# Routed activations of an expert layer: turned on VectorE and spread by ScalarE, where TensorE transposed them

## The reference, cut to what matters

```python
logits = xt @ W_router + routing_bias
scores, idx = jax.lax.top_k(jax.nn.sigmoid(logits), 2)
g = jnp.einsum('th,ehi->tei', xt, Wg_r)
u = jnp.einsum('th,ehi->tei', xt, Wu_r)
hmid = silu(g) * u
combined = jnp.einsum('tei,eih,te->th', hmid, Wd_r, wts)
```

## Time and profile before

| | us |
|---|---|
| median of 3 runs | 812.71 (811.16 to 813.40) |
| profiled execution, its own time | 809.95 |
| span from first to last instruction in it | 808.1 |
| PE busy in the span | 773.6 |
| DVE busy | 517.4 |
| ACT busy | 355.5 |
| POOL busy | 301.0 |

### The profile page before, as it was taken

The page is one execution under the profiler, slowest core; times in us unless marked ns, Lnnn a source line. Parts: engine busy times, 40 slices in busy tenths (PEclk is TensorE's granted clock), DMA queues, the critical chain, the costliest instruction groups (busy, mean ns, idle before and its releaser), DMA issues.

```text
span 808.1 us, 17427 instructions
## 1 busy us (share of the span) xinstructions
PE 773.6 (96%) x6752; PEld 574.0 (71%) x6753; DVE 517.4 (64%) x1125; ACT 355.5 (44%) x913; POOL 301.0 (37%) x157
## 2 busy tenths in 40 slices
PE   4799999999899999989999999899999999999996
PEld 3555455554657778878867877788888888888884
DVE  5799798788652447777788887855364333443335
ACT  4356545661443248852178768523432122211221
POOL 1000000000442833732032213533649999993034
PEclk9999999999899999999999999999999999999999
DMA  9968756683520050040388000030485355531138
GB/s 341 390 252 327 259 218 243 262 326 122 219 105 1 0 149 13 2 138 0 105 312 314 1 0 1 22 137 25 183 306 210 112 206 167 191 135 52 52 114 275
DMA packets 46576, 127.04 MB, mean 157 GB/s; under 512 B 4001, under 2 KB 8353, under 8 KB 40369
## 3 DMA queue, kind: packets, MB, share of 16 engines
q1 hardware_dynamic: 36752, 105.44, 35.9%
q10 hardware_dynamic: 7200, 12.32, 4.4%
q0 software_dynamic: 2560, 8.39, 3.1%
HBM read 101.99 MB, written 24.15 MB: 156 GB/s over the span
## 4 chain that ended last, share of the span: by engine, by line
PE 81%; DVE 5%; DMA 5%; POOL 3%; ACT 3%; issue 2%; SPq 0%; DVEq 0%; ACTq 0%; POOLq 0%
PE scores L611 11%; PE bank L641 11%; PE bank L1137 7%; PE bank L1139 7%; PE bank L1138 7%; DMA nat<-in_ctx_keys 3%; PE bank L691 2%; POOL picked L1379 2%; PE bank L845 2%; PE bank L693 2%; PE bank L851 2%; PE bank L692 2%; PE bank L846 2%; PE bank L626 2%; PE bank L881 2%
## 5 line engine op out<-in xcount | busy, mean ns | idle before, releaser
L1844 DVE STREAM_TRANSPOSE ctxT<-nat 128x1024 f32<-128x1024 f32 (+3 forms) x124 | 116.9, 1004 | 7.8 <-DMA nat<-in_ctx_keys 7.5
L641 PE MATMUL bank<-nat,probT 128*64 128x512 f32 (+1 forms) x416 | 93.9, 597 | 0.1
L1366 POOL TENSOR_TENSOR ring_lo<-ring_raw,ring_hi 128x2048 fp32r<-128x2048 f32 x18 | 83.0, 4611 | 14.5 <-ACT ring_hi L1732 13.3
L1244 POOL TENSOR_TENSOR wq_lo<-wq_raw,wq_hi 128x1024 fp32r<-128x1024 f32 x4 | 9.3, 2352 | 207.6 <-ACT wq_hi L1477 207.6
L1137 PE MATMUL bank<-ring_hi,xg_lo 128*128 x180 | 74.2, 412 | 0.0
L1139 PE MATMUL bank<-ring_hi,xg_hi 128*128 x180 | 70.6, 392 | 0.0
L1138 PE MATMUL bank<-ring_lo,xg_hi 128*128 x180 | 70.1, 389 | 0.0
L2488 DVE TENSOR_TENSOR rhm_lo<-bank,rhm_hi 128x512 fp32r<-128x512 f32 x21 | 14.5, 692 | 80.2 <-ACT rhm_hi L1743 80.2
L641 PEld LDWEIGHTS bank<-nat,probT 128*64 128x64 f32 (+1 forms) x416 | 27.9, 136 | 51.6 <-issue 48.1
L1749 ACT COPY hn<-bank 128x512 f32<-128x512 f32 x22 | 12.9, 588 | 112.0 <-PE bank L1139 112.0
L611 PE MATMUL scores<-ctxT,hn 32*64 32x416 f32 (+8 forms) x1536 | 55.2, 426 | 5.1 <-issue 2.7
(11 more groups left out here) (317 smaller groups left out, 1936.1 us busy)
## 6 DMA issues: line engine op xcount, KB each, us to landing
nat<-in_ctx_keys SPq DMA_DIRECT2D x48, 1024.0 KB, 8.1
ring_raw<-in_Wexp SPq DMA_DIRECT2D x21, 1024.0 KB, 6.3
x_slots<-zeros SPq DMA_DIRECT2D x1, 5632.0 KB, 18.2
y_slots<-zeros SPq DMA_DIRECT2D x1, 5632.0 KB, 32.7
hn<-x_slots ACTq DMA_DIRECT2D x22, 256.0 KB, 4.5
y_slots<-hn ACTq DMA_DIRECT2D x22, 256.0 KB, 3.0
w_raw<-in_Wexp SPq DMA_DIRECT2D x3, 1024.0 KB, 5.3
nat<-in_ctx_keys SPq DMA_DIRECT2D x16, 130.0 KB
```

What stands on the lines that cost most here:

```text
L641: last = nc.tensor.matmul(context_bank(k)[64 * b:64 * b + 64, :], probT[0:n, j, 64 * b:64 * b + 64], nat[k % 2][0:n, b, j, :], start=j == ...
L1366: last = nc.gpsimd.tensor_tensor(ring_lo[at], ring_raw[at], ring_hi.bitcast(F32)[at], ALU.subtract)
L1844: dve.transpose(dst, src).then_inc(columns_ready, 1)
```

## The change

For tiles 0 to 20 PE no longer transposes the hidden tile. Instead:

- DVE turns the 32x32 blocks of `rhm` with one STREAM_TRANSPOSE into `rhm_blocks`, straight behind the multiplication.
- ACT places the 16 blocks of rows and columns with 16 copies of 32 partitions x 4x32 elements into `rhmT`. They stand ahead of `output_rows(t - 1)`, where the one cast out of bank 3 stood behind it.
- DVE makes the high part with `tensor_copy` from `rhmT` (SBUF to SBUF), having waited also for `rdown_full` of tile t-1, and the low part with a TENSOR_TENSOR whose two inputs both lie in SBUF.

The last tile, 21, is done as before, through bank 3.

The core of the diff:

```diff
             def routed_hidden(t, par, at, turn=None):
-                if not (isinstance(t, int) and t < 2):
-                    hidden_columns(t - 1)
                 pe.wait_ge(xgT_ready, t + 1)
...
-                    if isinstance(t, int) and t == 1 and m == gate:
-                        hidden_columns(0)
...
             def hidden_columns_out(t):
-                act.wait_ge(rhmT_full, t + 1)
-                nc.scalar.copy(hidden_parts(t)[0][:].rearrange("p c q -> p (c q)"), bank[3][:]).then_inc(rhm_split, 1)
+                act.wait_ge(rhm_turned, 2 * t + 1)
+                if isinstance(t, int) and t == TILES - 1:
+                    last = nc.scalar.copy(rhm_last[0][:].rearrange("p c q -> p (c q)"), bank[3][:])
+                else:
+                    for g in range(4):
+                        for a in range(4):
+                            last = nc.scalar.copy(rhmT[B32 * a:B32 * (a + 1), :, B32 * g:B32 * (g + 1)],
+                                                  rhm_blocks[B32 * g:B32 * (g + 1), :, a, :])
+                last.then_inc(rhm_split, 1)
...
             def routed_step(t, par, turn, load=True):
...
-                    output_rows(t - 1, 1 - par, turn)
-                    hidden_columns_out(t)
+                hidden_columns_out(t)
+                output_rows(t - 1, 1 - par, turn)
...
                 dve.tensor_tensor(rhm[:], rhm[:], bank[2][:], ALU.mult).then_inc(rhm_ready, 1)
+                if not (isinstance(t, int) and t == TILES - 1):
+                    dve.wait_ge(rhm_ready, t + 1)
+                    dve.transpose(rhm_blocks[:].rearrange("p c a q -> p (c a q)"), rhm[:]).then_inc(rhm_turned, 1)
...
             def hidden_split(t):
                 dve.wait_ge(rhm_split, t + 1)
...
+                if not (isinstance(t, int) and t == 0):
+                    dve.wait_ge(rdown_full, t)
+                dve.tensor_copy(rhm_hi[:], rhmT[:]).then_inc(rhm_turned, 1)
+                dve.wait_ge(rhm_turned, 2 * t + 2)
+                dve.tensor_tensor(rhm_lo[:], rhmT[:], rhm_hi.bitcast(F32)[:], ALU.subtract).then_inc(rhmT_ready, 1)
```

More of the change, by code:

```diff
@@ L300, in perceiver_kernel @@
         rhm = place(172, "rhm", [P, D])
+        rhm_blocks = place(156, "rhm_blocks", [P, HC, 4, B32])
+        rhmT = place(158, "rhmT", [P, HC, P])
         rhm_hi = place(174, "rhm_hi", [P, HC, P], F32R)
@@ L348, in perceiver_kernel @@
         xg_loaded, y_stored = ([sem(f"{n}{i}") for i in range(2)] for n in ("xg_loaded", "y_stored"))
-        xgT_full, xg_split, xgT_ready, rgate_full, rup_full, rsilu_ready, rhm_ready, rhmT_full, rhm_split, rhmT_ready, rdown_full, yo_ready = (
-            sem(n) for n in ("xgT_full", "xg_split", "xgT_ready", "rgate_full", "rup_full", "rsilu_ready", "rhm_ready", "rhmT_full",
+        xgT_full, xg_split, xgT_ready, rgate_full, rup_full, rsilu_ready, rhm_ready, rhm_turned, rhm_split, rhmT_ready, rdown_full, yo_ready = (
+            sem(n) for n in ("xgT_full", "xg_split", "xgT_ready", "rgate_full", "rup_full", "rsilu_ready", "rhm_ready", "rhm_turned",
                              "rhm_split", "rhmT_ready", "rdown_full", "yo_ready"))
@@ L1161, in routed_hidden, with last_hidden_columns @@
                     routed_product(bank[b], m, at, xg_hi[par], xg_lo[par], full)
-                    if isinstance(t, int) and t == 1 and m == gate:
-                        hidden_columns(0)
                     if m == gate and turn is not None:
                         rows_columns(t + 1, 1 - par, turn)
[L1167 to L1172, removed]
+            def last_hidden_columns():
+                pe.wait_ge(rhm_ready, TILES)
                 for c in range(HC):
                     last = nc.tensor.transpose(bank[3][:, c * P:(c + 1) * P], rhm[:, c * P:(c + 1) * P], ident)
-                last.then_inc(rhmT_full, 1)
+                last.then_inc(rhm_turned, 1)
             def routed_output(t, par, at):
@@ L1223, in _ @@
             routed_hidden(TILES - 1, 1, at[1])
-            hidden_columns(TILES - 1)
+            last_hidden_columns()
             routed_output(TILES - 2, 0, at[0])
@@ L1765, in _ @@
             routed_silu(1)
+            hidden_columns_out(1)
             output_rows(0, 0, 0)
-            hidden_columns_out(1)
             def routed_step(t, par, turn, load=True):
@@ L1773, in routed_step @@
                 routed_silu(t)
-                if isinstance(t, int) and t == TILES - 1:
-                    hidden_columns_out(t)
-                    output_rows(t - 1, 1 - par, turn)
-                else:
-                    output_rows(t - 1, 1 - par, turn)
-                    hidden_columns_out(t)
+                hidden_columns_out(t)
+                output_rows(t - 1, 1 - par, turn)
             act.wait_ge(slots_ready, 4)
@@ L2483, in routed_mult @@
                 dve.tensor_tensor(rhm[:], rhm[:], bank[2][:], ALU.mult).then_inc(rhm_ready, 1)
+                if not (isinstance(t, int) and t == TILES - 1):
+                    dve.wait_ge(rhm_ready, t + 1)
+                    dve.transpose(rhm_blocks[:].rearrange("p c a q -> p (c a q)"), rhm[:]).then_inc(rhm_turned, 1)
             def hidden_split(t):
                 dve.wait_ge(rhm_split, t + 1)
-                hi, lo = hidden_parts(t)
-                dve.tensor_tensor(lo[:].rearrange("p c q -> p (c q)"), bank[3][:],
-                                  hi.bitcast(F32)[:].rearrange("p c q -> p (c q)"), ALU.subtract).then_inc(rhmT_ready, 1)
+                if isinstance(t, int) and t == TILES - 1:
+                    hi, lo = rhm_last
+                    dve.tensor_tensor(lo[:].rearrange("p c q -> p (c q)"), bank[3][:],
+                                      hi.bitcast(F32)[:].rearrange("p c q -> p (c q)"), ALU.subtract).then_inc(rhmT_ready, 1)
+                    return
+                if not (isinstance(t, int) and t == 0):
[3 more added lines that the diff above has]
+                dve.tensor_tensor(rhm_lo[:], rhmT[:], rhm_hi.bitcast(F32)[:], ALU.subtract).then_inc(rhmT_ready, 1)
             rows_columns_out(0, 0)
```

## The result

The changed kernel takes 873.46 us (median of 4 runs, 872.31 to 877.43), the kernel before 812.56 (811.16 to 813.4) on the same chip: 1.076 times as long, interval 1.0722 to 1.0798, or some 61 us more. The forecast was 881, range 834 to 900. The profiled execution took 872.87 us with a span of 871.1, 8 us under the sum.

A forecast was written before the change was run, and what follows sets the result against it. PE bounds the kernel before, at 9.11 us a tile; afterwards the DVE-ACT circle does. 602.2 to the first multiplication, 191.9 for 19 circles, 6.5, exclusions 46, then 32.7 and 1.85 make 881 us; 8-in-10 range 834 to 900.

The forecast's parts named there:

- the circle: DVE and ACT, from one tile's multiplication to the next: a closed chain of 10.10 us, longer than PE's 8.67.
- the exclusion: DVE's high and low part and POOL's splits exclude each other for whole instructions: 6.2 us a hit tile, 46 us in all.
- PE's transposes: Four on PE per hidden tile, 0.44 us; removing 21 times four, 9.2 us, gains nothing as PE stops being the bound.
- the upper bound, 17.5: Longest circle of a hit tile: four POOL instructions per circle, 17.5 us, 7.4 us more than the unhit circle.
- the bursts' edges: POOL's splits come in about four bursts of six; waits falling away where bursts begin or end take off 8 us.
- The turn and the multiplication: On DVE beside POOL: each reads one SBUF tensor, so priced at no wait; 18 us more if the turn waited too.
- From the multiplication of tile 19 to ACT's copy: End of the routed part: 6.5 us to ACT's copy of tile 18's product, with 32.7 us behind it.
- PE's clock: Rival: PE, idling 7 us in a 16 us circle, may fall to 1.2 GHz; adds nothing unless it lasts through the tile.
- no exclusion: Rival: DVE's high and low part do not wait for POOL's instructions; 835 us, chance 0.10.
- Overlapping copies: Rival: ACT's 16 copies overlap, 3.3 us for all; 848 us with exclusion, chance 0.10; 806 us without, chance 0.04.
- a wait in one request only: Rival: only one of DVE's two requests per tile waits for POOL, 25 us; 860 us, chance 0.09.
- passed over a second time: Rival: DVE is passed over at a POOL instruction boundary, each request waiting about twice, 76 us; 911 us, chance 0.07.

The follow-up runs named there:

- e2: Changed kernel with the turned hidden tile in PSUM bank 3, where ACT's copies write and DVE's high and low part read: 835.7 us, 1.0254 of before.
- e4: Kernel before, PE transposes kept, but ACT copies bank 3 to SBUF and DVE makes both parts from there: 853.89 us, 1.0445 of before.
- e6: e2 with PE turning the next rows ahead of the gate product and DVE making input rows while it waits for the copies: 817.69 us, 1.0079 of before.
- e7: e6 with ACT loading the input rows one step earlier, right after the SiLU: 817.66 us, 1.0077 of before.
- e10: e7, tile 18's product stored ahead of tile 19's copies, DVE's weight-split wait moved to the previous tile's turn, which PE's gate awaits: 807.31 us, 0.994 of before.
- e3: Changed kernel with ACT storing the previous tile's down product ahead of the 16 copies, except for the last tile: 928.03 us, 1.1398 of before.
- e9: e7, tile 18's product stored ahead of tile 19's copies, weight-split wait moved from DVE to PE ahead of the gate product: 811.78 us, 0.9998 of before.
- e5: Changed kernel with the edits of e2 and e3 together: 837.37 us, 1.0314 of before.
- e1: Changed kernel with each POOL split of a 128x2048 weight matrix made by four 128x512 instructions: 849.74 us, 1.0418 of before.

## Why the prediction was right

The mechanism was the forecast one, in both halves; e2 and e4 show the halves apart, and e6 that the circle is what sets the pace. The size of one half, the exclusion, was off by 8.5 us of 46.

- PE's transposes were called worth nothing while the circle is longer. Right: the circle of a quiet tile is 10.0 or 10.4 us. Once the circle is shorter (e6, e7, e10) the tile takes 8.62 us; the forecast figure for that was 8.67.
- The circle, 10.10 us forecast. By its terms at 735.90: multiplication, turn and handovers 1.46 (1.52), sixteen copies and handover 4.94 (4.94 for the copies), high and low part 1.15 (1.18), to the next multiplication 2.35 and, every second time, 2.85 (2.46). The last term is the one that alternates: where DVE's loop turns, it waits 0.64 us for its next instruction, 0.15 otherwise. Without the waits that leaves 191.4 for 19 circles, 191.9 forecast; in hit tiles that 0.5 is hidden. The copies do not overlap: 16 of 296 ns took 4.91 us, 0.307 each, so the rule of the Trainium skill that was weighed (ScalarE: Activation LUTs, section What ACT_TABLE_LOAD costs) does not hold for this kind.
- The exclusion, 46 us forecast, 37.5 measured: the term that was mis-sized, and the whole of the 8 us. A tile hit in both parts had the forecast price in the mean, 6.1 us for 6.2, from 4.6 to 7.5 in single tiles (low parts of 3.97 or 4.88 us in place of 0.69, by which of POOL's two instructions was ahead: 3.3 or 4.2 us; high parts 0.4 to 4.2 us more). But seven tiles were hit in the high part and six in the low, where 8.7 were forecast. The first three are hit one after the other in lock-step with POOL (635.72 - 618.80 = 16.92 us, four POOL instructions, as in the upper bound, 17.5). After that, from 661.56 on, POOL works in seven bursts of two or four instructions and not in four of six: the three of four hit one tile each, and of the four of two only the first touched a high part, by 0.67 us. The 8 us taken off for the bursts' edges would have had to be 16.5.
- The turn and the multiplication at their usual time beside POOL: right, at most 716 and 689 ns.
- From the multiplication of tile 19 to ACT's copy 6.39 (6.5), and 32.4 (32.7) from there. Right.
- PE's clock: forecast to fall and to cost nothing. It fell (0.50 from 616 to 620, 0.83 from 640 to 660), and beside the sum there is no room for a cost. e3 shows the other side of "unless it lasts through the tile": as soon as an instruction of the circle waits for the slow product, it does cost.
- The first multiplication came 1.24 us later than before (603.46), which no term had; it is in a part of the program that the change doesn't touch, and in the other runs it comes at 602.86 (e9) to 608.09 (e5).
- One reading of the kernel before was wrong without harm. The cast that the low part waited for did not come early:

```profile
654.12 0.69 DVE L2483 TENSOR_TENSOR rhm<-rhm,bank 128x512 f32<-128x512 f32 x1 [0.45 <-PE bank L1139]
658.79 0.69 DVE L2488 TENSOR_TENSOR rhm_lo<-bank,rhm_hi 128x512 fp32r<-128x512 f32 x1 [3.98 <-ACT rhm_hi L1743]
```

DVE stood idle for 3.98 us there, where it idles 4.98 to 5.07 for the copies now, and elsewhere only 0.45 us ahead of the multiplication and 0.80 ahead of the input rows. So DVE's way from one multiplication to the next had about 1.2 us to spare in PE's 9.11. One more DVE instruction of 0.43 us fits in, as e4 shows (quiet tiles of 9.11 us); the turn, the high part and a longer wait do not.

Of the rivals, no exclusion (835) is what e2 built; its 835.7 us meet that figure in part by luck, for there the copies are shorter by 0.035 us each and the high part longer by 0.26. Overlapping copies and a wait in one request only are ruled out by the rows above, and no high or low part is passed over a second time.

## What to carry to other kernels

Before taking work from the engine that is the bound, add up the closed circle that the work goes into, with every handover and with the instructions that merely stand between on the same queue; here 4.9 us of small copies per tile, in the middle of a circle, stood against 0.44 us per tile that TensorE was spared. If GpSimd works in long instructions, let VectorE's critical casts and two-input instructions read from PSUM, as in e2, or cut GpSimd's instructions, as in e1. When a step is moved to fill an idle gap, look for the waits that it carries: the one for another tile's weights cost 9.7 us at its new place, and 4 when put where it is due.

## What the runs showed of the hardware that was not expected

- A ScalarE copy of 32x128 from SBUF takes 296 ns into SBUF and 261 into PSUM, 0.307 and 0.271 us apart, so neither overlaps with the next. Two ScalarE casts of 128x2048 from SBUF to SBUF, 1.91 us each, took 3.71 together in the changed kernel (at 601.24), so it is not reading SBUF that rules an overlap out; why the small ones have none is open.
- VectorE's cast of 128x512 to SBUF takes 0.43 us from SBUF and 0.69 from PSUM. Reading PSUM was the slower form by 0.26 us and still the better choice beside GpSimd.
- After 5.65 us of standing still TensorE ran a whole down product at the lower level (granted clock 0.50 in e3), 0.43 us a matmul against 0.23, and was back at full speed right behind it.
- With two more register values loaded on TensorE in a loop turn (five and not three), every turn took 0.96 us longer with TensorE as the bound; with the three that were there before, the tiles with and without the loop's turn take the same 8.62 us.
